# Query and key stacks copied to every third partition, and the first group's projections, sign transposes and weight loads in another order

## The reference, cut to what matters

```python
def bitnet_linear(x, weight, scale_param):
    s = jnp.maximum(jnp.mean(jnp.abs(weight), axis=1), 1e-08)
    binary_w = jnp.sign(weight / s[:, None])
    y = jnp.einsum('bsi,oi->bso', x, binary_w)
    return jnp.nan_to_num(y * (s * scale_param)[None, None, :], ...)
q = bitnet_linear(hidden_states, q_weight, q_scale)   # 32 heads of 32
k = bitnet_linear(hidden_states, k_weight, k_scale)   # 8 heads of 32, each for 4 query heads
v = bitnet_linear(hidden_states, v_weight, v_scale)
scores = jnp.einsum('bhqd,bhkd->bhqk', q, k) / np.sqrt(HEAD_DIM)
out = jnp.einsum('bhqk,bhkd->bhqd', jax.nn.softmax(scores, axis=-1), v)
x = x + bitnet_linear(out, o_weight, o_scale)
x = x + xattn(layernorm(x), ctx_4096)
x = x + ffn(layernorm(x))
```

## Time and profile before

| | before |
|---|---|
| median of 3 runs | 1464.37 us |
| the profiled execution | 1468.78 us, its span 1467.0 us |
| granted TensorE clock, mean | 0.992 |
| TensorE matmuls busy | 1354.5 us, 92% of the span |
| VectorE, ScalarE, GpSimd busy | 62%, 48%, 35% |

### The profile page before, as it was taken

One profiled execution on the slowest core, in us unless ns is written; L12 is line 12 of the kernel. 1 busy time (PEld: TensorE's weight loads), 2 busy tenths in 40 slices (PEclk: granted clock), 3 DMA queues, 4 the chain that ended last, 5 costly groups with the idle time before them and its releaser, 6 DMA issues.

```text
span 1467.0 us, 22531 instructions
## 1 busy us (share of the span) xinstructions
PE 1354.5 (92%) x8377; PEld 962.5 (66%) x8377; DVE 915.4 (62%) x1612; ACT 709.9 (48%) x1589; POOL 514.9 (35%) x448
## 2 busy tenths in 40 slices
PE   6788999899989998899889898878999999999999
PEld 4555455546555555557667677656888888888887
DVE  5578556836673667667577485664664764674576
ACT  4375603550454045417657476564564454354452
POOL 2047513761476146702121121122442342342330
PEclk9999999999999999999999999999999999999999
DMA  5785555565547555265536354544510310210202
GB/s 150 143 168 131 111 99 117 95 102 109 109 74 112 106 119 121 88 200 148 148 94 185 110 141 119 131 112 157 184 62 0 115 58 1 105 69 1 101 0 101
DMA packets 95105, 157.62 MB, mean 107 GB/s; under 512 B 9942, under 2 KB 49172, under 8 KB 94996
## 3 DMA queue, kind: packets, MB, share of 16 engines
q1 hardware_dynamic: 94996, 156.17, 43.8%
HBM read 82.21 MB, written 25.17 MB: 73 GB/s over the span
## 4 chain that ended last, share of the span: by engine, by line
PE 67%; DVE 11%; DMA 9%; issue 5%; ACT 5%; SPq 2%; POOL 1%; DVEq 0%; POOLq 0%; ACTq 0%
PE bank L1032 15%; PE bank L1045 8%; PE bank L947 7%; DMA q_stack<-hi_lo 5%; PE bank L819 5%; PE bank L1058 3%; PE bank L932 3%; PE bank L775 3%; PE bank L868 3%; PE bank L853 3%; PE bank L833 2%; PE bank L905 2%; PE bank L1016 2%; PE bank L794 2%; PE bank L883 2%
## 5 line engine op out<-in xcount | busy, mean ns | idle before, releaser
L1611 POOL TENSOR_TENSOR fold<-wide 128x512 f32<-128x512 f32 x128 | 164.4, 1293 | 248.5 <-ACT wide L1113 222.3
L1113 ACT ACTIVATE wide<-bank 128x512 f32<-128x512 f32 x256 | 151.2, 597 | 145.7 <-PE bank L853 143.3
L1402 DVE TENSOR_REDUCE neg_top<-bank 128x2 f32<-128x512 f32 x256 | 170.9, 680 | 55.7 <-PE bank L833 54.3
L1665 POOL TENSOR_TENSOR v_lo<-v_all,v_hi 128x512 fp32r<-128x512 f32 (+1 forms) x88 | 124.0, 1410 | 232.4 <-ACT v_hi L1219 232.4
L853 PE MATMUL bank<-q_stack,k_stack 98*128 98x512 f32 x256 | 138.9, 543 | 2.8 <-ACT wide L1113 2.4
L1032 PE MATMUL bank<-pT_hi,v_hi 128*128 128x512 f32 x344 | 134.2, 390 | 1.5 <-POOL v_lo L1665 1.5
L1032 PE MATMUL bank<-pT_hi,v_lo 128*128 128x512 f32 x344 | 134.1, 390 | 0.0
L1032 PE MATMUL bank<-pT_lo,v_hi 128*128 128x512 f32 x344 | 133.8, 389 | 0.0
L833 PE MATMUL bank<-k_stack,q_stack 96*128 96x256 f32 x512 | 111.6, 305 | 14.8 <-DMA q_stack<-hi_lo 9.2
L1130 ACT ACTIVATE wide<-bank,neg_max 128x256 f32<-128x256 f32 x256 | 119.8, 487 | 7.3 <-DVE neg_max L1430 7.3
L833 PEld LDWEIGHTS bank<-k_stack,q_stack 96*128 96x128 f32 x512 | 93.6, 194 | 42.9 <-DMA q_stack<-hi_lo 14.1
(11 more groups left out here) (186 smaller groups left out, 3113.7 us busy)
## 6 DMA issues: line engine op xcount, KB each, us to landing
q_stack<-hi_lo SPq DMA_DIRECT2D x96, 256.0 KB, 6.0
xin<-x_scratch SPq DMA_DIRECT2D x33, 512.0 KB, 4.6
xq_stack<-xhi_lo SPq DMA_DIRECT2D x128, 128.0 KB, 2.4
x_res<-in_x SPq DMA_DIRECT2D x21, 512.0 KB, 4.3
x_scratch<-x_res SPq DMA_DIRECT2D x16, 512.0 KB, 2.7
xin<-in_ctx SPq DMA_DIRECT2D x16, 512.0 KB, 4.2
x_group<-x_scratch SPq DMA_DIRECT2D x32, 256.0 KB, 3.4
x_scratch<-x_group SPq DMA_DIRECT2D x32, 256.0 KB, 2.4
```

Source lines behind the costliest of these rows:

```text
L1113: act.activation(PT[m % PT_RING][:, :], tiles[m % 2][:, :], ACT.Exp).then_inc(sem["tile_exped"], 1)
L1402: dve.tensor_reduce(neg_top[U % 2][:, r, b, :], tops[n % 2][:, :].rearrange("p (a b) -> p a b", a=QT), AX.X, ALU.max, negate=True).then_in ...
L1611: pool.tensor_tensor(fold[f % FOLD_RING][:, :], PT[2 * f % PT_RING][:, :], PT[(2 * f + 1) % PT_RING][:, :], ALU.add).then_inc(sem["folded" ...
L1665: pool.tensor_tensor(inner_home(W, 1), inner_gu(f, n), as_f32(inner_home(W, 0)), ALU.subtract).then_inc(sem["iw_lo"], 1)
```

## The change

Two things. The three copies of a stack no longer go to partitions 0 to 31, 32 to 63 and 64 to 95; copy a goes to partitions a, a+3, a+6 and so on up to 95, in the key stack and in the query stack alike. And group 0 has another order of sign transposes, weight loads, value projections, the first `top` and the second key projection, with five more loads in `AFTER_STACK`. The helper `with_inside` becomes `inside`, which can put steps behind several parts.

```diff
-    order += signs(VB + 1) + flip_sign(VB) + [("diag_v",)] + with_inside(q_parts(0, 0), 4, flip_sign(VB + 1))
-    order += signs(1) + [("wload", QB + 1), ("v", 0, 0), ("v", 0, 1), ("row_v", 0), ("row_v_out", 0)]
-    order += [("v_out", 0, 0), ("v_out", 0, 1)] + flip_sign(1) + signs(2) + [("wload", 3)]
-    order += with_inside([part + [score(0, c)] for c, part in enumerate(q_parts(0, 1))], 4, flip_sign(2))
-    order += signs(QB + 1) + [("wload", 4)] + top(0)
-    order += with_inside(q_parts(0, 2), 4, flip_sign(QB + 1)) + signs(3) + [("wload", 5)] + key(0, 1)
-    order += flip_sign(3) + signs(4) + [("wload", OB)]
-    order += with_inside([part + [score(0, UH + c)] for c, part in enumerate(q_parts(0, 3))], 4, flip_sign(4))
+    order += signs(VB + 1) + flip_sign(VB) + [("diag_v",)]
+    order += inside(q_parts(0, 0), {4: flip_sign(VB + 1)}) + signs(1) + [("wload", QB + 1), ("v", 0, 0)]
+    order += flip_sign(1) + signs(2) + [("wload", 3), ("v", 0, 1), ("row_v", 0), ("row_v_out", 0), ("v_out", 0, 0)]
+    order += [("wload", 4), ("v_out", 0, 1)]
+    order += inside([part + [score(0, c)] for c, part in enumerate(q_parts(0, 1))],
+                    {1: flip_sign(2), 3: signs(QB + 1), 6: flip_sign(QB + 1)}) + [("wload", 5)]
+    order += inside(q_parts(0, 2), {1: signs(3), 3: top(0), 6: flip_sign(3)}) + signs(4) + [("wload", OB)]
+    order += key(0, 1)
+    order += inside([part + [score(0, UH + c)] for c, part in enumerate(q_parts(0, 3))], {4: flip_sign(4)})
...
-               | {("wload", OB + i) for i in range(1, KB)})
+               | {("wload", OB + i) for i in range(1, KB)} | {("wload", i) for i in (2, 3, 4, 5, QB + 1)})
...
-                        sp.dma_start(kst[a * HD:(a + 1) * HD, kt * (P // HD):(kt + 1) * (P // HD), :].bitcast(F32),
+                        sp.dma_start(kst[a:SUB:3, kt * (P // HD):(kt + 1) * (P // HD), :].bitcast(F32),
...
-                        sp.dma_start(qst[U % Q_STACKS][a * HD:(a + 1) * HD, :, :].bitcast(F32),
+                        sp.dma_start(qst[U % Q_STACKS][a:SUB:3, :, :].bitcast(F32),
```

More of the change, by code:

```diff
@@ L117, in self_order @@
     score = lambda g, i: ("pre", g * GROUP_HEADS + i)
-    with_inside = lambda parts, k, extra: [p for c, part in enumerate(parts) for p in part + (extra if c == k else [])]
+    inside = lambda parts, extra: [p for c, part in enumerate(parts) for p in part + extra.get(c, [])]
     order = [("ones",), ("scales",), row(0), ("wload", QB), row(1), row(2), row(3), ("scales_out",)]
```

## The result

The changed kernel takes 1447.9 us (median of 4 runs, 1445.87 to 1449.71), the kernel before beside it 1466.11 us (4 runs, 1464.28 to 1472.02). The ratio is 0.9862, with a 95% interval from 0.9834 to 0.9889: 1.4% faster. The profiled execution took 1447.79 us, 21.0 us less than that of before (1468.78). The medians lie 18.2 us apart. Two executions in the experiments' rounds ran far slower than all others (2496 us in e6, 2686 us in the kernel before beside e5 to e8); medians and ratios of experiments leave them out.

A forecast was written before the change was run, and what follows sets the result against it. Matmuls fill 92% of the span, so only TensorE's waits, largest for query stack copies, were worth anything; 10.0 + 1.7 + 8.1 - 0.5 - 1.2 = 18.1 us, from 1464.37 to 1446 us, range 1438 to 1460.

The forecast's parts named there:

- the likeliest case: Whole kernel: interleaved copies take 1.0 to 1.5 us each, giving 1446 us, range 1438 to 1452; chance 0.66.
- Copies at 205 GB/s: Stack copies: interleaved ones run at 205 instead of 125 GB/s, 1.25 us each, so a set lands some 2.5 us earlier.
- the two bounds: Stack copies: 125 GB/s if the number of partitions written counts, at best 397 GB/s if their range counts.
- Rival 2: Stack copies stay at 2.1 us and the new waits only move idle time: 0 to 3 us gained; chance 0.10.
- The eleven waits: Self-attention behind group 0: ten TensorE waits for query stacks and one for a key stack go, 10.0 us gained.
- The surcharge of 0.16 us a wait: Score matmuls behind stack waits: each wait costs 0.16 us more than the idle time the trace gives.
- The half-clock stretch at 417: Self-attention behind the longest of these stack waits: 3.4 us at clock 0.50; 1.7 us returns if the fall follows the wait.
- First score: Group 0: `q_stack0` lands earlier, so the first score comes at 43.5 instead of 47.84, 4.3 us gained.
- The rest of the first group: `top`'s wait gone +1.9, tile 3's sign wait gone +1.7, VectorE's later work -2.2, late `q_stack2` with its scatter -0.5 us.
- The clock in the first group: Eight rounds of projection and scores at clock 0.51: 2.4 us returns, less 1.2 in case it falls all the same.
- 5 to 6: Changed profile: key stack copies land in 5 to 6 us, against a median of 8.9 us before.
- Rival 4: Slower: interleaved pieces collide more, a copy takes over 2.2 us, paid at 11 waits and 21 other sets; chance 0.05.

The follow-up runs named there:

- e6: The changed kernel with `top` put back ahead of the third query projection and tile 3's signs between key and fourth query projection: 1449.56 us, ratio 0.9868.
- e5: The changed kernel with the second value half and the values' scaling put back ahead of tile 1's transposed signs: 1447.46 us, ratio 0.9849.
- e8: The changed kernel with only the query stacks' copies interleaved, the key stack's in blocks; scores not the reference's: 1451.21 us, ratio 0.9875.
- e4: A kernel without the computation, only 256 KB SBUF copies at different partition steps: 128, 129, 233 and 380 GB/s at steps 1 to 4.
- e2: The changed kernel's order and held loads, with copies back in blocks of 32 partitions: 1472.78 us against 1470.19 before, ratio 1.0007.
- e7: The changed kernel with only the key stack's copies interleaved, the query stacks' in blocks; scores not the reference's: 1463.87 us, ratio 0.9957.
- e9: The changed order with copies in blocks and without the five held weight loads: 1467.4 us against 1468.94 before, ratio 0.9985.
- e10: The changed kernel again, without an edit: 1449.83 us, ratio 0.9864 to the kernel before.
- e3: The changed kernel without SP's five new waits before weight loads: 1448.92 us, ratio 0.9854 to the kernel before.
- e1: The kernel before with the interleaved copies alone, first group's order and loads kept: 1455.39 us against 1470.19, ratio 0.9908.

## Why the prediction was right

It said 1446 us (1438 to 1460), and 1447.9 was measured; the likeliest case came about. That the medians' difference (18.2 us) meets the 18.1 so closely is luck: between the two profiled executions it is 21.0, and single runs differ by several microseconds. By its own steps, on the traces (20.8 us from the span's start to the last tile matmul, 607.9 less 587.1; 18.1 were forecast):

- **Copies at 205 GB/s.** Right in effect, a little low: every third partition goes at 220 to 233 GB/s alone (e4). Of the two bounds given for it, the range of partitions written fell as a reason: a range of 64 at step 2 gains nothing. So did the statement that the rate rises with the number of partitions written, which the rows could not part from the range. Rival 2 (the number of partitions, or the ports of a set taken together) fell with the same run.
- **The eleven waits, 10.0 us.** The rest of self-attention gains 10.8 in the changed kernel, 10.6 with the query stacks alone, 10.5 with all copies in the old order, and at most 1.8 without the query stacks. The surcharge of 0.16 us a wait goes the right way; if all 10.8 belong to the eleven waits, it is some 0.07 us short.
- **The half-clock stretch at 417, 1.7 us.** Borne out by these traces, though that the fall followed from the wait is not shown. The stretch behind the 1.6 us wait is gone in all seven profiles without such waits, and it cost 1.7 us by the windows above. It stands in the one profile of the kernel before alone, though: in e2, e7 and e9, where the same wait is 0.5 to 0.6 us, it is missing too, and in e2 a wait of 1.5 us eight tile matmuls earlier had no stretch behind it. What the forecast left out is that the other stretches come and go between executions: with them the net is 0.3 us (7.9 less 7.6), and -3.3 in the execution of e10.
- **First score, 4.3 us.** 4.7 behind the key stack's issue. Landings came as worked out: 35.6 for 35.8, 43.0 for 43.5.
- **The rest of the first group: +1.9, +1.7, -2.2, -0.5,** together 0.9 us. The first tile gained 8.1 us; less 4.7 and the 2.5 of the clock this is 0.9, but the agreement is partly luck. e6 shows the first two together as 2.9 instead of 3.6. The fourth did not come as told: `q_stack2` lands at 64.6 for 65.2 and nothing waits for it; of the 0.6 us of e3, 0.4 are already in the first score. That leaves, by difference, some 1.8 us for VectorE's pace instead of 2.2, in line with the 1.7 that it gives back in e5.
- **The clock in the first group, 2.4 less 1.2 for the chance that it falls all the same.** It did not fall there in the changed kernel's two profiles, nor in e3: 2.5. It fell at 43.6 to 46.5, in the wait or up to 1.6 us behind it, in each kernel in which TensorE waited 3.3 to 5.7 us at a time there (before, e1, e2, e5, e7, e8, e9), and in none that waited under 1 us; in e6 it fell at 50.29, behind a wait of 1.9.
- **Not in the sum:** from the first to the ninth tile matmul 11.4 us instead of 12.9. The copies bring it: e1, with the old order, has 11.4 as well, and so has e8 with the query stacks alone. Two waits of before are gone there, 0.34 us for copied signs and 0.25 for `top_rows`; what the rest consists of is open.
- **A landing was mis-sized:** key stack copies in "5 to 6" us; their median is 3.9. The 5.6 us from 29.89 to 35.5 are the set's, from its first issue on; the forecast had worked out the set and called it a copy. Rival 4 counts 21 sets besides the 11 waited for; the 120 copies are 40 sets, so there are 29.

Added up: 10.8 + 0.3 + 4.7 + 0.9 + 2.5 + 1.5 = 20.7 us, for 10.0 + 1.7 + 4.3 + 0.9 + 1.2 and nothing for the last. The clock behind the first group came 1.4 us short, and the other terms 4.0 over.

The two parts are not a sum. At the ninth tile matmul the copies alone gain 3.2 us, the order alone loses 4.0, both together gain 9.6; with the halved clock taken out it is 3.6, -1.7 and 7.1. The prediction's rival 2 described this well (stacks landing at 48.0 and near 73, against 48.17 and, in e2, a score waiting until 75.8), but gave the order 0 to 3 us where it has -4.0 at the ninth tile. What e2 adds is `top_rows` behind the held load.

## What to carry to other kernels

When SBUF copies into few partitions bound a wait, measure the rate at another partition step before touching the order of work: 32 rows written at step 3 went 1.8 times as fast as at step 1, step 2 brought nothing, and step 4 went 3 times as fast in the run that only copies (in the kernel it was not tried). An order of work is tuned to its transfers' landings, so an order that is worth 6 us with copies at step 3 can cost 4 with copies in blocks at the same point of the trace; test the two parts of such a change apart. Where a gain of 3 us is in question and runs differ by 7, read it as a distance between two events of the trace, with the halved clock taken out, rather than from the totals. And compare stretches of halved clock between two kernels by the matmuls ahead of them, not by the time at which they stand.

## What the runs showed of the hardware

The rate of SBUF copies from 128 to 32 partitions at the same DMA share (1.02 to 1.08) is 128, 129, 233 and 380 GB/s at steps 1, 2, 3 and 4: nothing at step 2, then 1.8 and 3 times. Taking the stack waits out of TensorE's stream behind the first group took one stretch at 1.2 GHz away and left the others: seven profiles without such waits (changed, e1, e3, e5, e6, e8, e10) lost 3.4 to 11.2 us there, the kernel before 7.9. But for two of them (417.70 before, 151.62 in e10) the stretches of all eleven profiles stand at four places of the program, behind 781 to 797, 1793 to 1813, 2761 to 2781 and 3672 to 3680 matmuls, each place in 7 to 10 of the profiles, for 3.4 or 6.8 us. TensorE transposes the next rows there and waits, 1.5 us for `hT_lo` at the first three places and 1.8 to 2.0 us for `actT_lo` at the fourth:

```profile
131.21 1.12 PE L776 MATMUL bank<-ident,x_res 128*128 128x128 f32 x4 [1.51 <-DVE hT_lo L1324]
```

Each fall behind the first group, the two others too, lies inside a wait of 1.5 to 2.0 us or up to 1.7 us behind its end; but 9 of the 44 such waits at the four places had no stretch. No run took those waits away, so it is open whether the stretches would go with them. In the first group, where a wait of 3.3 us or more went, the stretch behind it went too.
